# Long convolution: a complex product of three real ones, channels in two halves, lags from oldest to newest, a PSUM bank for every stage

## The reference

```python
xz = jnp.einsum('bld,ed->bel', hidden_states, W_in)      # W_in (1024, 256)
x, z = jnp.split(xz, 2, axis=1)                          # 512 channels each
xp = jnp.pad(x, ((0, 0), (0, 0), (D_CONV - 1, 0)))       # D_CONV = 4
xc = conv_b[None, :, None]
for j in range(D_CONV):
    xc = xc + conv_w[None, :, j, None] * xp[:, :, j:j + Lq]
x = _silu(xc)
x_f = jnp.fft.rfft(x, n=2 * Lq)
k_f = jnp.fft.rfft(k_ssm, n=2 * Lq)                      # k_ssm (512, 1024)
y = jnp.fft.irfft(x_f * k_f[None], n=2 * Lq)[..., :Lq]
y = (y + x * D_skip[None, :, None]) * _silu(z)
return jnp.einsum('bhl,dh->bld', y, W_out)               # hidden_states = layernorm(x)
```

## Time and profile before

| what | us |
|---|---|
| median of 3 runs (13695.54 to 13703.24) | 13702.88 |
| the profiled execution: its time | 13691.93 |
| the profiled execution: its span, first to last instruction | 13690.1 |
| of it the filter phase, from its DMA issue to its last DVE instruction | 11131.03 to 11177.58 |
| of it the convolution phase, from PE's first to DVE's last instruction | 11187.03 to 11948.76 |

### The profile page before, as it was taken

One profiled execution on the slowest core, in us unless ns is written; L12 is line 12 of the kernel. 1 busy time (PEld: TensorE's weight loads), 2 busy tenths in 40 slices (PEclk: granted clock), 3 DMA queues, 4 the chain that ended last, 5 costly groups with the idle time before them and its releaser, 6 DMA issues. The chain is left out here.

```text
span 13690.1 us, 221161 instructions
## 1 busy us (share of the span) xinstructions
PE 5931.4 (43%) x52626; PEld 4318.2 (32%) x52626; DVE 10113.9 (74%) x54550; ACT 8412.6 (61%) x42691; POOL 228.4 (2%) x293
## 2 busy tenths in 40 slices
PE   7222222222222222222222222222367766678998
PEld 6222222222222222222222222222344444453335
DVE  3777777777777777777777777777738638846874
ACT  4666666666666666666666666666636421153665
POOL 0000000000000000000000000000000000012000
PEclk8555555555555555555555555555579978887999
DMA  1100100000010010001001000000000000001100
GB/s 46 20 13 13 20 13 13 16 17 13 13 20 13 13 20 13 13 13 20 13 13 20 13 13 17 16 13 13 15 12 0 3 22 0 1 32 45 29 25 20
DMA packets 339791, 227.11 MB, mean 17 GB/s; under 512 B 27666, under 2 KB 324571, under 8 KB 338272
## 3 DMA queue, kind: packets, MB, share of 16 engines
q1 hardware_dynamic: 338528, 213.50, 7.3%
HBM read 187.61 MB, written 25.43 MB: 16 GB/s over the span
## 5 line engine op out<-in xcount | busy, mean ns | idle before, releaser
L526 PE MATMUL scan_p_car<-scan_hs,scan_mean_mat 32*32 32x2 f32 x16392 | 576.8, 198 | 6839.4 <-DVE scan_hb L653 6827.4
L526 PEld LDWEIGHTS scan_p_car<-scan_hs,scan_mean_mat 32*32 32x32 f32 x16392 | 400.8, 135 | 7018.3 <-DVE scan_hb L653 7006.2
L571 ACT ACTIVATE scan_act_ps<-scan_act_ps 128x64 f32<-128x64 f32 (+1 forms) x8193 | 1642.1, 200 | 64.6
L571 ACT ACTIVATE scan_act_ps<-scan_r 128x64 f32<-128x64 f32 x2048 | 466.2, 228 | 1876.2 <-DVE scan_r L650 1876.2
L553 PE MATMUL scan_p_y<-scan_c_masked,scan_hb 128*64 128x4 f32 x16384 | 1234.2, 253 | 0.0
L531 PE MATMUL scan_p_car<-scan_eps_row,ones 1*128 1x3 f32 x4102 | 1198.1, 360 | 38.6 <-DMA scan_a_log<-L_attn_a_A_log 38.5
L571 ACT ACTIVATE scan_cm<-scan_dl,scan_s 128x64 f32<-128x64 f32 x2049 | 712.3, 348 | 728.1 <-DVE scan_s L676 728.1
L650 DVE TENSOR_TENSOR scan_c<-scan_V,scan_cm 128x64 f32<-128x64 f32 x4096 | 739.2, 222 | 467.8 <-ACT scan_cm L571 422.7
L553 PEld LDWEIGHTS scan_p_y<-scan_c_masked,scan_hb 128*64 128x64 f32 x16384 | 1055.4, 216 | 34.3
L531 PEld LDWEIGHTS scan_p_car<-scan_eps_row,ones 1*128 1x128 f32 x4102 | 1020.5, 308 | 71.5 <-DMA scan_a_log<-L_attn_a_A_log 38.9
L653 DVE SCALAR_TENSOR_TENSOR scan_uw<-scan_w,scan_rsq 128x64 f32<-128x64 f32 x2048 | 462.0, 226 | 657.5 <-ACT scan_rsq L571 652.0
(11 more groups left out here) (445 smaller groups left out, 17926.6 us busy)
## 6 DMA issues: line engine op xcount, KB each, us to landing
scan_step_in<-scan_scratch SPq DMA_DIRECT2D x520, 256.0 KB, 6.1
qk_scratch<-qkv_parts SPq DMA_DIRECT2D x32, 384.0 KB, 2.5
attn_qT<-qk_scratch SPq DMA_DIRECT2D x192, 64.0 KB, 2.2
attn_kT<-qk_scratch SPq DMA_DIRECT2D x192, 64.0 KB, 2.2
scan_scratch<-prep_dts SPq DMA_DIRECT2D x32, 256.0 KB, 2.1
x<-L_attn_a_x SPq DMA_DIRECT2D x1, 4096.0 KB
out<-x SPq DMA_DIRECT2D x1, 4096.0 KB
filter_taps<-c_kT SPq DMA_DIRECT2D x1, 2048.0 KB
```

The costliest lines, as they stand in the source:

```text
L526: last = nc.tensor.matmul(p_car[slot][rows, 0:2], mean_mat[rows, :], hs[rows, :], start=False, stop=True)
L571: nc.scalar.activation(dst, src, func, **kw).then_inc(counts[par]["act"], 1)
```

## The change

- **Three forms for two.** The forward matrix has three columns of 128 for each `mt`: real + imaginary, real, imaginary (`FORMS` = 3). The filter phase makes for each lag the real part G0, imaginary - G0, and imaginary + G0, by two more DVE instructions of 128 x 1024 a lag. A lag then needs three real products, not four.
- **Channels in halves.** The unit of work is one block of one half of the channels (`CW` = 256): `UNITS` = 32 units, half by half, within a half sequence by sequence, in one loop with no drain between. A lag's product and addition have 128 x 1536 elements, both `mt` in one.
- **Lags from oldest to newest.** The lag that needs the newest block's spectrum is multiplied last; `gated` of the unit before stands after the third lag.
- **A bank for every stage.** `p_x`, `p_i`, `p_g`, `p_t`, `p_o` and three `p_f` of one bank each. `xT` has two buffers, and ACT in place of POOL copies its three halo columns (a new instruction of 128 x 6).

The core of the diff:

```diff
@@ long_filter_phase, DVE
+                    dve.wait_ge(summed, 6 * l + 4)
+                    nc.vector.tensor_tensor(spectra[:, l, :, 1, :], turned[:, l, :, :], spectra[:, l, :, 0, :], ALU.subtract).then_inc(summed, 1)
+                    nc.vector.tensor_tensor(spectra[:, l, :, 2, :], turned[:, l, :, :], spectra[:, l, :, 0, :], ALU.add).then_inc(summed, 1)
@@ convolution_phase, PE
+                for n in range(-2, UNITS + 1):
+                    if inside(n - 1):
+                        pe.wait_ge(z_made, 2 * n)
...
+                        for ct in range(CU):
+                            for mt in range(2):
+                                for c in range(2):
+                                    last = nc.tensor.matmul(p_i[:, ct, :], z_spec[:, mt, c, ct * P:(ct + 1) * P], inverse[:, mt, c, :], ...
...
+                        project(n - 1, CH, p_g).then_inc(g_done, 1)
+                    if inside(n + 1):
+                        pe.wait_ge(u_done, n + 2)
...
+                                last = nc.tensor.transpose(p_t[:, t, ct * P:(ct + 1) * P], u[:, ct, t * P:(t + 1) * P], env["ident"][:, :])
+                    if inside(n + 2):
...
+                        project(n + 2, 0, p_x).then_inc(x_done, 1)
+                    if inside(n + 1):
+                        pe.wait_ge(rows_done, n + 2)
+                        for q in range(2 * FORMS):
...
+                                last = nc.tensor.matmul(p_f[q // 2][:, q % 2, :], forward[:, k, q // FORMS, q % FORMS, :], rows_u[:, k, :], ...
+                    if inside(n - 1):
+                        pe.wait_ge(y_done, n)
...
+                                last = nc.tensor.matmul(p_o[:, t, :], gate[:, k, t * P:(t + 1) * P], w_out[:, h * CU + k, :], ...
@@ convolution_phase, DVE
-                        source = spec[:, (i - l) % RING, mt, :, :].unsqueeze(1).to_broadcast([P, 2, 2, CH])
-                        factor = G[:, l, mt, :, :].unsqueeze(2).to_broadcast([P, 2, 2, CH])
...
-                    nc.vector.tensor_tensor(z_spec[:, mt, 0, :], total[:, 0, 0, :], total[:, 1, 1, :], ALU.subtract).then_inc(multiplied, 1)
+                for n in range(-1, UNITS):
+                    if inside(n + 1):
...
+                                nc.vector.scalar_tensor_tensor(u[:, ct, :], xT[:, m % 2, ct, j:j + NB], conv_w[:, c, j:j + 1], u[:, ct, :],
...
+                    if inside(n - 2):
+                        add(n - 2)
+                    if inside(n):
...
+                        for idx in range(count):
+                            l = count - 1 - idx
+                            dve.wait_ge(f_copied, (n - l + 1) * BANKS)
...
+                            nc.vector.tensor_tensor((term if idx else total)[:, :, :, :], spec[:, (i - l) % RING, :, :, :], G[:, l, :, :, h * CW:(h + 1) * CW],
+                                                    ALU.mult).then_inc(multiplied, 1)
...
+                            if inside(n - 1) and idx == min(2, count - 1):
+                                gated(n - 1)
...
+                        nc.vector.tensor_tensor(z_spec[:, :, 0, :], total[:, :, 0, :], total[:, :, 2, :], ALU.subtract).then_inc(z_made, 1)
+                        nc.vector.tensor_tensor(z_spec[:, :, 1, :], total[:, :, 0, :], total[:, :, 1, :], ALU.add).then_inc(z_made, 1)
```

More of the change, by code:

```diff
@@ L1869, in _ @@
                             for k in range(BT):
-                                last = nc.tensor.matmul(p_k[q % 8][:, :], forward[:, k, mt, c, :], taps[:, l * BT + k, :], start=(k == 0), stop=(k == BT - 1))
+                                last = nc.tensor.matmul(p_k[q % 8][:, :], forward[:, k, mt, 1 + c, :], taps[:, l * BT + k, :], start=(k == 0), stop=(k == BT - 1))
                             last.then_inc(k_done, 1)
@@ L2006, in _ @@
+                for n in range(-2, UNITS + 1):
+                    if inside(n - 1):
+                        pe.wait_ge(z_made, 2 * n)
+                        if n - 1:
+                            pe.wait_ge(y_done, n - 1)
+                        for ct in range(CU):
                             for mt in range(2):
                                 for c in range(2):
-                                    for k in range(BT):
-                                        last = nc.tensor.matmul(p_f[mt * 2 + c][:, :], forward[:, k, mt, c, :], rows_u[:, k, :], start=(k == 0), stop=(k == BT - 1))
@@ L2010, in _ @@
-                                    last.then_inc(f_done, 1)
+                                    last = nc.tensor.matmul(p_i[:, ct, :], z_spec[:, mt, c, ct * P:(ct + 1) * P], inverse[:, mt, c, :],
+                                                            start=(mt + c == 0), stop=(mt + c == 2))
+                        last.then_inc(i_done, 1)
+                        if n - 1:
+                            pe.wait_ge(gate_done, n - 1)
+                        project(n - 1, CH, p_g).then_inc(g_done, 1)
@@ new lines, in _ @@
+                    if inside(n + 1):
+                        pe.wait_ge(rows_done, n + 2)
+                        for q in range(2 * FORMS):
+                            if n + 1 and q % 2 == 0:
+                                pe.wait_ge(f_copied, (n + 1) * BANKS - BANKS + q // 2 + 1)
+                            for k in range(BT):
+                                last = nc.tensor.matmul(p_f[q // 2][:, q % 2, :], forward[:, k, q // FORMS, q % FORMS, :], rows_u[:, k, :], start=(k == 0), stop=(k == BT - 1))
+                            if q % 2:
+                                last.then_inc(f_done, 1)
@@ new lines, in _ @@
+                    if inside(n - 1):
+                        pe.wait_ge(y_done, n)
+                        if n - 1:
+                            pe.wait_ge(added, n - 1)
+                        h = place(n - 1)[0]
+                        for t in range(BT):
+                            for k in range(CU):
+                                last = nc.tensor.matmul(p_o[:, t, :], gate[:, k, t * P:(t + 1) * P], w_out[:, h * CU + k, :], start=(k == 0), stop=(k == CU - 1))
+                        last.then_inc(o_done, 1)
@@ L2118, in convolution_layer @@
+                add(UNITS - 2)
+                gated(UNITS - 1)
+                add(UNITS - 1)
 def convolution_layer(nc, env):
```

277 lines of the change are left out of this document (122 added, 155 removed).

## The result

Before and after on one chip, four runs each: 13701.22 us (13695.54 to 13703.24) and 13528.75 us (13516.88 to 13539.45). The ratio is 0.9875, 95% interval 0.9857 to 0.9892: 172.5 us less. The forecast was 13550, in a range of 13524 to 13600; the median lies in that range, 5 us above its lower end, and outside the inner band of 13535 to 13570.

What follows compares the result with a forecast made beforehand. DVE was taken as the bound mid-sequence; in the first blocks DVE and PE waited for each other. The phase falls from 761.7 to 602.8 us (158.9 less), the filter phase adds 5.9: 13550 us, range 13524 to 13600.

Steps and rivals of the forecast that it cites:

- fill and first three steps: Start of the convolution phase: 25.7 us from empty until PE's first inverse, then 14.4 + 14.4 + 15.2; 69.7 us.
- first four steps of the other sequences: Three later sequence starts: three PE steps of 14.4, one of 15.2 and 3.1 for a cold start, 61.5 us each.
- filter part: Filter phase ahead of the convolution: ten more DVE instructions (4.9 us) and a larger forward matrix (1.0), 5.9 us more.
- unit of five lags: Middle of each sequence, DVE the bound: 20.94 us a unit; two units 41.9 for 50.8 before.
- dense step of PE: First three steps of a sequence: PE's work without waits at full clock sets the step, 14.4 us.
- fourth step: Fourth step of a sequence: DVE's `add` waits for PE's output projection, then DVE's work follows; 15.2 us.
- cold start: At a sequence's start, PE works at a lower clock after the idle end of a DVE-bound step: 3.1 us lost.
- B: Rival: the first steps run at a mixed PE clock, 18.3 us for 14.4; 46 us given back, 13596 us; chance 0.17.
- C: Rival: PE becomes the bound everywhere, at 1.2 GHz throughout with steps of 28.8 us; 13907 us; chance 0.02.
- D: Rival: DVE's products of 1536 elements cost what 2048 did; about 98 us given back, 13648 us; chance 0.04.
- E: Rival: no cold start and overlapping hand-overs, 13 us less, 13537 us; chance 0.04 beyond the forecast's low side.
- overlooked chain: Rival: a missed dependency, with DVE idle before the gating, some 3 us in each of 32 steps; chance 0.03.

Runs made afterwards that it cites:

- experiments 8 and 9: Changed kernel with half of the forward transform's matmuls left out (8): 13504.96 us; with the last of DVE's three taps left out (9): 13519.62 us.
- experiment 7: Changed kernel with the addition to x moved from ahead of the first lag to behind the third, just ahead of the gating: 13514.08 us.
- experiment 1: Changed kernel with four real products again (two forms), while halves, order of lags, banks and the one loop stay: 13608.9 us.
- experiment 2: Changed kernel with the lags taken from newest to oldest: 13528.32 us.
- experiment 6: Changed kernel with PE's projection behind the forward transform, and ACT's spectrum copies ahead of the projection's copies: 13554.42 us.
- experiment 3: Changed kernel with the gating behind the last lag: 13542.88 us.

## Why the prediction was right

What bounds each stretch was right, and the phase was forecast at 602.8 us and is 596.0. Of the 21 us between forecast and median, eight lie in the forecast's own terms and the rest in code that the change doesn't touch. That the median is still within the range, 5 us above its lower end, is in part luck: the profiled execution, 13516.88 us, lies below that end. The terms of the sum, in us:

| term | forecast | measured |
|---|---|---|
| fill and first three steps | 69.7 | 70.3 |
| first four steps of the other sequences, three times | 184.5 | 180.0 |
| 16 units of five lags | 335.0 | 333.5 |
| end | 13.6 | 12.3 |
| phase | 602.8 | 596.0 |
| filter part | +5.9 | +4.7 |

- **The unit of five lags** was forecast at 20.94 us and is 20.99. The last one is 18.6: it has no taps to do for a unit behind it, which my sum of 16 equal units overlooked. That DVE is the bound there is shown by experiments 8 and 9.
- **The dense step of PE** was 14.4 and is 14.25, the fourth step 15.2 and is 15.3. That the fourth is held by `add` is shown by experiment 7. Its own price was right, but the wait also took DVE's lead for the fifth step, so that it costs 3.1 us a sequence where I saw one.
- **The cold start** was priced at 3.1 us by a row in which PE had waited 9.46. In the new kernel PE waits 3.9 to 4.8 ahead of that step, and the loss is 1.8 to 2.2. This term was mis-sized, and is 3.6 of the 6.8 us of the phase. The shorter wait isn't shown to be the reason: in the same trace a wait of 3.63 us was followed by a loss of 2.7, one of 6.45 by a loss of 1.5.
- **The filter part** grew by 4.7 for 5.9, and by 6.3 against experiment 1, which has its own profile. The difference between the two is within the scatter of the filter part, 2.3 us, so the runs don't size this term any better.
- **The rest** of the difference lies in code that the change doesn't touch. Ahead of the layer the profiled executions differ by 10.2 us (the filter's DMA is issued at 11131.03 before and at 11120.84 after), behind it by 3.8. Over the profiles of the eleven experiments that moment lies between 11121.1 and 11139.5, although the code ahead of it is the same in all. So this is scatter between runs, and I take no cause for it. On another chip the kernel of experiment 2, whose phase is the changed kernel's to 0.1 us, lies 163.2 us below the kernel before (13691.48 to 13528.32), near the 161.0 that phase and filter part account for.

The rivals. **B** is refuted: the first four steps run at a granted clock of 0.97, the cold start included, though each step writes all eight banks, and at 1.00 in the stretch of experiment 6, waits and all. What the Trainium skill ("TensorE: Matmul & The Clock Gate", "A second HAM failure mode: psum-queue depth-cycling") tells of another kernel, clock swings by idle bits between groups, doesn't occur in these dense steps. The row from which I drew it, 8.83 us for a forward transform, lies behind 2.12 and 1.18 us of waiting around 1.09 us of work; the fill of experiment 6 shows the same slow forward transform behind waits and transposes. **C** falls with it: the mean step is 18.0 us ((596.0 - 26.5 - 12.3) / 31), below the 23.1 from which it decides. **D** is refuted by 1756 ns for 1536 elements. **E**, hand-overs that overlap and no cold start, is wrong in its mechanism, though its 13537 lies nearest the median, which is luck: the cold starts are there, at 1.8 to 2.2 us in place of 3.1. The overlooked chain isn't there: no five-lag unit has a wait in it.

Each part of the change, as far as the runs tell it: three products for four 86 us of the phase, less 6 in the filter part; halves, order and banks together 79.5. Within these the inverse's bank alone is worth 62 and a loop without drains 48.5, with the drains and the sharing each put back alone. They aren't parts of one sum, since each was taken back from a kernel that has all the others, and the kernel before had one drain between its sequences, not three. Channels in halves were not tried alone: for a whole block `p_x` takes two banks, and a buffer for every stage would need more than eight.

## What to carry to other kernels

Write down for each stretch which engine sets the step, and price a change there alone: 14% more work for PE (the third form of the forward transform) cost nothing where DVE was the bound, and 1.7 us a step where PE was. Of the two stages whose bank was taken back, it paid for the one whose buffer the slowest engine reads late, and not for the other; to find such a stage, ask who frees the buffer and when in its step. Put a wait that can't be avoided as late as possible on the engine that is about to become the bound: in experiment 7 the lead that it kept was worth 2.1 us a sequence, and the wait itself 1.1.

## What was not expected of the hardware

- A wait that is hidden in time can still cost by the clock. After 6.55 us without work the next 8 records of PE took 3.78 us and the next 16 took 4.34, for 1.89 and 3.62 dense (experiment 3). After 0.90 us the 16 records of an inverse took 3.72 for 3.62, and waits of 0.74 us in each step left the granted clock at 1.00 (experiment 6).
- How long the wait was doesn't tell what is lost behind it. Two pairs of rows, the first from the kernel before, the second from the changed one, all with 16 records:

```profile
11285.83 5.41 PE L1970 MATMUL conv_p_z<-xnT,conv_w_in 128*128 128x256 f32 x16 [2.06 <-DVE x L2098]
11322.79 3.72 PE L1970 MATMUL conv_p_z<-xnT,conv_w_in 128*128 128x256 f32 x16 [2.05 <-DVE x L2098]
...
11272.82 5.13 PE L1986 MATMUL conv_p_i<-convolution_inverse,conv_z_spec 128*128 128x256 f32 x16 [6.45 <-DVE conv_z_spec L2124]
11314.82 6.31 PE L1986 MATMUL conv_p_i<-convolution_inverse,conv_z_spec 128*128 128x256 f32 x16 [3.63 <-DVE conv_z_spec L2124]
```

The same wait of 2.05 us cost 1.8 us once and 0.1 once, and a wait of 6.45 cost less than one of 3.63. Behind equal waits of 6.44 or 6.45 us the inverse of the changed kernel took 5.13, 6.58, 6.14 and 5.93. A cold start is therefore better priced by a range, here 1.5 to 3.0 us behind waits of 3.6 to 6.5, than by one row.

- Four transposes in the midst of matmuls, 0.43 us from start to start of the next, did not slow what came behind them: the projection behind them took 1.89 us, as elsewhere.
